# Back pipeline of a language-model tower: roots of the norms moved within the step, third norm's rows ahead of the key-value norm

## The reference

```
h = h + _L0_ffn_ref(...)                     # gate weights x expert outputs
x = _layernorm(h)                            # second norm ("x2")
qkv = x @ W_qkv.T + b_qkv                    # 16 heads of 4
k, v = norm(k), norm(v)                      # w * (k - mean) / (std + eps) + b
kv = einsum('bhnd,bhne->bhde', k, v) / HW     # HW = 256 rows
out = q @ kv ; ret = out + x ; h = h + gelu(ret @ W_proj.T + b_proj) + x
x = _layernorm(h)                            # third norm ("x3")
weights = x @ wr + br                        # route: the best 127 of 256 rows
h = h + x ; h[best] += mlp(x[best]) * weights[best]
```

## Time and profile before

| | us |
|---|---|
| median of 3 runs | 5102.29 (5095.44 to 5108.06) |
| the profiled execution | 5105.13 |
| its span, first to last instruction | 5103.3 |
| back pipeline, 4632 to 5060 us | 428.0 |
| in it PE, DVE, ACT, GpSimd busy | 321.8, 339.5, 336.0, 169.4 |
| last part (route selection, final sums) | 43.3 |

### The profile page before, as it was taken

The page is one execution under the profiler, slowest core; times in us unless marked ns, Lnnn a source line. Parts: engine busy times, 40 slices in busy tenths (PEclk is TensorE's granted clock), DMA queues, the critical chain, the costliest instruction groups (busy, mean ns, idle before and its releaser), DMA issues. The chain is left out here.

```text
span 5103.3 us, 63233 instructions
## 1 busy us (share of the span) xinstructions
PE 3049.3 (60%) x21149; PEld 2316.2 (45%) x21149; DVE 2806.5 (55%) x5784; ACT 2360.4 (46%) x4288; POOL 2219.9 (44%) x2218
## 2 busy tenths in 40 slices
PE   3646663666566565565565565565565565644775
PEld 2435552554454454454454454454454454433443
DVE  8857882454454454454454454454454454558985
ACT  3635665444344444344444344444344444405885
POOL 7766613334434434434434434434434434336530
PEclk7767665777777777777777777777777777766886
DMA  2111101111111111111111111111111111112101
GB/s 58 25 21 20 22 7 44 24 23 30 28 23 30 28 23 32 26 23 30 28 23 34 24 23 30 28 23 34 24 24 29 28 24 30 22 47 55 45 12 33
DMA packets 157528, 145.13 MB, mean 28 GB/s; under 512 B 71240, under 2 KB 133080, under 8 KB 156776
## 3 DMA queue, kind: packets, MB, share of 16 engines
q1 hardware_dynamic: 88656, 109.49, 6.4%
q0 software_dynamic: 68768, 34.45, 6.2%
HBM read 92.97 MB, written 50.82 MB: 28 GB/s over the span
## 5 line engine op out<-in xcount | busy, mean ns | idle before, releaser
L937 PE MATMUL es_pgot<-hash_space,es_pick 128*128 128x256 bf16 x13056 | 1834.3, 288 | 1425.3 <-issue 1404.9
L857 POOL DMA_INDIRECT es_got<-node_table,late x1632 | 1548.1, 949 | 2127.2 <-DVEq L1077 1649.9
L937 PEld LDWEIGHTS es_pgot<-hash_space,es_pick 128*128 128x128 bf16 x13056 | 1300.4, 101 | 1901.6 <-issue 1743.9
L1019 DVE TENSOR_TENSOR es_prod<-es_pgot,es_own 128x512 f32<-128x512 f32 x272 | 187.7, 690 | 1799.4 <-PE es_pgot L937 1626.6
L871 ACT ACTIVATE es_pick<-es_away,consts 128x512 bf16<-128x512 f32 x1088 | 680.0, 711 | 7.1 <-DMA es_away<-sorted_keys 6.7
L293 POOL DMA_INDIRECT fr_ring<-in_emb,fr_rows x384 | 451.5, 1176 | 211.7 <-issue 112.8
L875 ACT ACTIVATE es_pick<-es_pick,consts 128x4096 bf16<-128x4096 bf16 x136 | 503.6, 3703 | 0.9
L894 ACT ACTIVATE ex_hid<-ex_phid,weights 128x256 f32<-128x256 f32 x128 | 53.6, 470 | 690.3 <-PE ex_phid L944 689.9
L1039 DVE TENSOR_TENSOR es_hot<-es_iota,late 128x1024 bf16<-128x1024 f32 x272 | 331.7, 1220 | 35.3 <-DVE es_st L1079 25.7
L1040 DVE TENSOR_TENSOR es_hot<-es_iota,late 128x1024 bf16<-128x1024 f32 x272 | 330.4, 1215 | 0.0
L894 ACT ACT_TABLE_LOAD x32 | 41.1, 1283 | 570.2 <-PE ex_phid L944 570.2
(11 more groups left out here) (351 smaller groups left out, 4302.3 us busy)
## 6 DMA issues: line engine op xcount, KB each, us to landing
es_away<-sorted_keys SPq DMA_DIRECT2D x68, 512.0 KB
es_got<-node_table,late POOLq DMA_INDIRECT x1632
edge_states<-es_st SPq DMA_DIRECT2D x68, 384.0 KB
expert_outputs<-ex_y SPq DMA_DIRECT2D x64, 256.0 KB
bk_y<-expert_outputs SPq DMA_DIRECT2D x8, 2048.0 KB
fr_ring<-in_emb,fr_rows POOLq DMA_INDIRECT x384
out_dram<-h SPq DMA_DIRECT2D x4, 1024.0 KB, 5.1
late<-in_edges SPq DMA_DIRECT2D x1, 2048.0 KB, 9.2
```

What stands on the lines that cost most here:

```text
L857: pool.indirect_dma_start(out=got[:, r, k, :], out_offset=None, in_=table_dram, in_offset=bass.IndirectOffsetOnAxis(ap=src[:, n, k:k + 1]. ...
L937: mm = pe.matmul(p_got[:, q, c * 256:c * 256 + 256], pick[:, r, q // 2, k, at * P:at * P + P], parts[:, part, k], start=(k == 0 and part = ...
```

## The change

In the back pipeline only the order within the lists changes. ACT: the root of `sd` and its Identity are issued in the step whose sums they need (`new`), ahead of `qt`, and no longer at the start of the next step; the third norm's root follows its squares at the end of the step; `norm_root` and `gate_root` stand at the end of step q=2 and no longer in q=3. DVE: x3 stands directly behind x2; part 0 of the gates stands behind the norm of keys and values. PE: the product of keys and values stands behind the turn of x3.

```
@@ scalar
-                if is_slot(normed):
-                    act.wait_ge(s_var, normed + 1)
-                    a.activation(sd[:], sd[:], ACT.Sqrt, scale=1.0 / (C1 - 1)).then_inc(s_sd, 1)
-                if is_slot(mlp):
-                    act.wait_ge(s_sum3, (mlp + 1) * ST)
-                    a.activation(rstd3[:, slot(mlp)], rstd3[:, slot(mlp)], ACT.Sqrt, scale=1.0 / D, bias=C("eps")).then_inc(s_std3, 1)
-                if is_slot(normed):
-                    act.wait_ge(s_sd, normed + 1)
-                    a.activation(sd[:], sd[:], ACT.Identity, bias=C("eps")).then_inc(s_std, 1)
-                if q == 3 and g + 1 < GN:
-                    norm_root(g + 1)
-                if q == 3 and g + 2 < GN:
-                    gate_root(g + 2)
...
                 if q == 3 and g + 2 < GN:
                     gate_exp(g + 2)
                 if is_slot(new):
+                    act.wait_ge(s_var, new + 1)
+                    a.activation(sd[:], sd[:], ACT.Sqrt, scale=1.0 / (C1 - 1)).then_inc(s_sd, 1)
+                    act.wait_ge(s_sd, new + 1)
+                    a.activation(sd[:], sd[:], ACT.Identity, bias=C("eps")).then_inc(s_std, 1)
+                if is_slot(new):
                     act.wait_ge(s_q_p, new + 1)
...
                         a.activation(sq3[:, t], xc[:, col], ACT.Square, accum_out=rstd3[:, col:col + 1]).then_inc(s_sum3, 1)
+                    act.wait_ge(s_sum3, (joined + 1) * ST)
+                    a.activation(rstd3[:, slot(joined)], rstd3[:, slot(joined)], ACT.Sqrt, scale=1.0 / D, bias=C("eps")).then_inc(s_std3, 1)
+                if q == 2 and g + 1 < GN:
+                    norm_root(g + 1)
+                if q == 2 and g + 2 < GN:
+                    gate_root(g + 2)
@@ vector: order in a step
 x2(new)
-gates_at(q, 0, g)
-norm(normed)
-x3(mlp)
+x3(mlp)
+norm(normed)
+gates_at(q, 0, g)
 gates_at(q, 1, g); mask(normed); sums(new); join(joined); gates_at(q, 2, g)
@@ tensor: order in a step
 turn x2, keys and values (new)
-product(normed)
 turn x3 (mlp)
+product(normed)
 second matrix (last); output (normed); ...
```

More of the change, by code:

```diff
@@ L1629, in _ @@
                     v.tensor_tensor(x2[:, new % 2], by_half(xc[:, slot(new)]), by_half(spread(rstd2[:, slot(new)], D)), ALU.mult).then_inc(s_x2, 1)
-                gates_at(q, 0, g)
+                if is_slot(mlp):
+                    dve.wait_ge(s_std3, mlp + 1)
+                    do(v.reciprocal(rstd3[:, slot(mlp)], rstd3[:, slot(mlp)]))
+                    if mlp >= 2:
+                        dve.wait_ge(s_hx3, mlp - 1)
+                        dve.wait_ge(s_x3_p, mlp - 1)
+                    v.tensor_tensor(x3[:, mlp % 2], by_half(xc[:, slot(mlp)]), by_half(spread(rstd3[:, slot(mlp)], D)), ALU.mult).then_inc(s_x3, 1)
                 if is_slot(normed):
@@ L1710, in _ @@
                     mm.then_inc(s_kv_p, 1)
[L1711 to L1717, removed]
                 if is_slot(mlp):
@@ L1729, in _ @@
                     mm.then_inc(s_w_p, 1)
+                if is_slot(normed):
+                    pe.wait_ge(s_kv, normed + 1)
+                    if normed >= 1:
+                        pe.wait_ge(s_rt, normed)
+                    for half in range(2):
+                        mm = pe.matmul(p_kvm, halves(normed)[:, half, 0:P], halves(normed)[:, half, P:2 * P], start=(half == 0), stop=(half == 1))
+                    mm.then_inc(s_kvm_p, 1)
                 if is_slot(last):
```

## The result

The changed kernel took 5133.3 us, median of five runs (5122.71 to 5145.12), against 5102.29 (5095.44 to 5108.53) on the same chip: a ratio of 1.0063 [1.0049, 1.0076], slower, 31 us. The forecast was 5124, its range 5096 to 5144. The profiled execution of the changed kernel took 5122.71, the shortest of its five, since the part ahead of the back stage happened to be 13.5 us shorter in it. So I compare the stage itself, from DVE's first instruction in it to its last ahead of the route selection, in the timelines of DVE.

A forecast was written before the change was run, and what follows sets the result against it. The prediction took the back stage to be bound by a loop of hand-overs, no engine full. Full groups +19.5 us, first group +3, last eight steps nothing, drain -0.8: together +22, so 5124 us, range 5096 to 5144.

The forecast's parts named there:

- q=2: Gated step where the next group's squares wait for part 0 and x3 waits out GpSimd's add: 15.3 us.
- q=3: Gated step with scores, scale and pick on DVE and the exponential's load on ACT: 14.35 us.
- five full groups: Full groups of four steps in the back stage: 55.2 us each against 51.3, together +19.5.
- q=0: Gated step with weights and outputs, 3.65 us of gate work on DVE: 12.8 us in all.
- ACT's tail: ACT's work from table load through small root and hand-over, now all ahead of DVE's next x3: 4.05 us.
- a late projection on PE: PE's projection waits for `qt`, 2.0 us later; said to fit beside the squares and cost nothing.
- q=1: Gated step with total and join, 3.6 us of gate work on DVE: 12.75 us in all.
- the norm behind x3: DVE's fixed part per step: x3 0.55 us, then the norm's four instructions 3.04, together 3.6.
- mask to table load: From DVE's masking of the product to ACT's table load behind `rt`, in each step: 1.5 us.
- (a): Rival, faster: roots come early enough that DVE never waits, a group is 48 us, 5082; chance 0.13.
- (b): Rival, same: squares' wait hidden and lock doesn't bite in q=2, group 53.35, +11 us, 5113; chance 0.18.
- (c): Rival, worse: x3 behind GpSimd's add in every gated step, or PE's projection late, 5140 us; chance 0.11.

The follow-up runs named there:

- Experiment 5: Changed kernel with the group's squares on ACT moved behind those of keys and values: 1.0039 of the kernel before, stage 505.6 us.
- experiment 9: Changed kernel with PE's order of before (product of keys and values ahead of the turn of x3): 1.0099 of the kernel before, stage 519.9 us.
- Experiment 6: Changed kernel with GpSimd's add of x3 ahead of its second pair of gathers: 1.003 of the kernel before, stage 505.7 us.
- 10: Changed kernel with both edits of Experiment 5 and Experiment 6 together: 1.0025 of the kernel before, stage 495.9 us.
- experiment 7: Changed kernel with twelve filler multiplications on PE ahead of its wait for the mask: 1.0057 of the kernel before, stage 520.1 us.
- experiment 1: Kernel before with only ACT's list changed, DVE and PE as before: 0.9966 of the kernel before, stage 475.2 us.
- experiment 4: Changed kernel with the norm ahead of x3 on DVE, gate part 0 still behind both: 0.998 of the kernel before, stage 477.7 us.
- experiment 3: Changed kernel with gate part 0 put back ahead of x3 and the norm: 1.0006 of the kernel before, stage 492.3 us.
- experiment 11: As 8, with the group's squares also ahead of x3's copy on ACT: 0.9952 of the kernel before, stage 471.8 us.
- 8: As experiment 1, with the squares of keys and values ahead of x3's copy on ACT: 0.9975 of the kernel before, stage 471.5 us.

## Why the prediction was right, and where it was 9 us short

*The mechanism was right.* The forecast of 5124 was made of a stage that is 22 us longer; it was 31.0. By its terms: five full groups +29.1 where 19.5 was said; the first steps +3.5 for 3; the last eight steps -0.5 for nothing; the drain -1.1 for -0.8. So the error is 9.6 us in the full groups. That the other terms hold to half a us is in part luck, for these stretches are cut at the reciprocal of `sd`, which the change itself moves within a step: cut at the mask (L1648, now L1646), the groups are again +29.0, but the first steps +4.3, the last eight -1.8 and the drain -0.5.

*What held, step by step.* x3 and norm from x3's start to the end of the norm: 3.60 in q=0, said 3.6. ACT's tail from table load to the root's arrival on DVE: 4806.86 - 4802.88 = 3.98, said 4.05. q=0: 12.8 in three groups of five, said 12.8 (13.3 in the other two, of which below). q=2: 15.2, said 15.3, with both of its parts: the squares start 6.1 behind x3, DVE's reduction waits 1.53 for the ones of keys and values behind them, and x3's product takes 0.97 for 0.42 beside the add of x2. Experiment 5 takes the first part away and gains 1.6 in q=2. In the group shown ACT came to L1388 later than the 3 us that were said, since `xt`'s copy had waited 2.6 for the turn of x2, which stood behind a late projection on PE, as the prediction had thought possible and priced at nothing. DVE waits for the squares of keys and values only in q=2 to speak of, so that price was right. The turn taken off the path was 0.8 in six steps, 4.8; experiment 9 has it at 3.4. DMAs cost nothing: no wait for one shows in the waits view of these groups.

*What failed.* q=1 was said to be 12.75 and q=3 14.35; they were 13.1 to 14.1 and 15.3 to 15.8 but once (14.4). The term of the sum that was mis-sized first is the norm behind x3, in the sentence that GpSimd's add "runs beside the reciprocal of `sd`". I looked at when x3 is ready and at the add's length, and not at what stands ahead of the add on GpSimd. Two gathers do. In q=1 and q=3, where x3 follows x2 soon, the add comes 2 us later, beside the two passes that read both inputs from SBUF, and these take 1.15 + 1.09 for 2 x 0.69: +0.86. That is so in three q=1 steps and four q=3 steps of the five groups; in two more q=1 steps, where the add is 1.35 late and not 2.1, it is 0.33. Together 6.7 us. The changed kernel has its own counter-case: in the last full group's q=3 no gathers are left, the passes take 0.69, and the step is the 14.4.

The second is mask to table load: 2.0 for 1.5, where the output product takes 1.22 and not 0.70. I had read the 1.5 from one q=3 step; in the kernel before, the product took 0.91 to 1.22 in each q=1 step of the full groups. In the changed kernel it is 1.22 in six of these groups' fifteen steps q=0, 1 and 3 (three times in q=1, twice in q=0, once in q=3), 0.52 each, 3.1 us. There PE's granted clock was at the lower level, 0.50, that is 1.2 GHz, before the mask and behind it. Windows of the changed kernel, the stretch up to the mask and what follows:

```profile
4799.00:4801.20 2.20, 1.45 (x8) 0.43 (x4) 2.02 (x4) 0.47 (x1) 1.29 (x1) 0.50 0.17 24
4801.20:4807.50 6.30, 6.28 (x21) 4.28 (x22) 3.90 (x9) 4.25 (x15) 2.37 (x3) 0.50 1.02 329
```

0.86 + 0.5 is the 1.4 by which q=1 is long in the group shown; over the five groups q=1 and q=3 are together 1.8 long on the mean, 9.2 of the 9.6 us. Experiment 6 is the test of the first term: it moves only that add, and its mean group is 55.35, where the prediction had 55.2.

Whether the clock fell because of the 0.86 us is not shown. In the step of 14.1 PE stood idle for 1.58 us until the slow passes were done (ahead of L1726), in experiment 6's step for 0.70, and ahead of the output product for 0.77 in both; in both the clock was 0.50 until the mask, and only in experiment 6's step was it 0.95 from there (4838.7 to 4840.5). By counts, of fifteen steps: six, seven and five have the product at 1.22 in the kernels that keep the slow passes (changed, experiments 5 and 9), two and three in those that don't (6 and 10). That leans toward a link; but two of the changed kernel's six are q=0 steps, which have no slow pass, and experiment 7 failed to tell the clock's share apart.

The Trainium skill (SBUF — State Buffer, Who interferes with whom) has DVE instructions with two SBUF inputs contend with GpSimd's reads. The trace agrees in both places, 0.97 for 0.42 and 1.15 for 0.69; the prediction used it at one place, where the same rule gives the other one too. As a lock that one side holds for the whole of its instruction, which is how the prediction has it, the second meeting doesn't read: DVE's pass began 0.48 us ahead of the add (4794.99 and 4795.47), and both were long, 1.15 for 0.69 and 1.25 for 0.72.

*The rivals.* (a), the roots early enough that DVE never waits, fell: DVE waits 5.8 us a group at x3. Its idea holds on the other order of DVE: there experiment 1 gains 10.3, but in the steps without gates, not in the groups. (b) fell: L1388 waits in q=2 (7.3 us in four groups, 3.1 at the longest, 0.5 in the one shown) and the hold-up of x3's product is there. (c) said that hold-up in more steps than one, for 5140; it came in two more steps of four, on the norm's passes and not on x3's product. The time of 5133 lies between my sum and (c), and the measured time alone would not have told them apart.

*What costs most, seen from the experiments.* Two orders of DVE: x3 ahead of the norm makes the norm wait for the later of two roots (experiment 4, which takes 38.8 away, the slow passes among it), and part 0 of the gates behind the norm holds up the mask and the squares (experiment 3: 24.3). The first undone is more than the whole loss, the second undone leaves 6.8.

## What to carry to other kernels

Move a result's producer earlier by all means, but in an in-order list put first what depends on the result that is ready first: x3 ahead of the norm gave away the earlier root of `sd`, and ACT's half alone was the better kernel. When two pieces of work on two engines hold each other up where they meet, look up the start of the second by its whole queue, not by when its input is ready: a 0.72 us add behind two gathers made DVE's passes 0.86 us longer in a step, and moving it was worth 10.8 us of the stage. When a term is read from one step, read it in the others too: mask to table load was 1.5 in the one and 2.0 in six of fifteen. When a wait has been removed, read off what is late next, before expecting the whole of it: after the roots it was the squares of keys and values, and with those moved too the gated groups were as long as before (256.4 and 256.5 us for five), with DVE busy for 90%.

## What was not expected of the hardware

In the third set all kernels, the one before included, ran in 3391 to 3443 us instead of 5090 to 5161. The back stage was the same (471.8 against 471.5 for experiments 11 and 8); the difference lies in the edge stream, a part that no kernel here changes. The row of the kernel before in the first run profiled, and of experiment 11 in the third set, from the page's groups of instructions:

```profile
L937 PE MATMUL es_pgot<-hash_space,es_pick 128*128 128x256 bf16 x13056 | 1834.3, 288 | 1425.3 <-issue 1404.9
```

```profile
L937 PE MATMUL es_pgot<-hash_space,es_pick 128*128 128x256 bf16 x13056 | 1517.5, 278 | 16.6 <-ACT es_pick L875 16.6
```

PE stood idle for 1405 us between these multiplications with nothing in the profile that released it, and for 17 us in the other session. Its cause stays open; the three sets ran on three different chips, so chip and session can't be told apart. Ratios of that set are larger for the same number of us, so its kernels are compared by the stage.
